# Reordering TensorE and the opening of a Mamba scan stage: eight weight parts, softplus behind the second gate, the second batch's rows normalized sooner

## The reference

```python
xz = layernorm(x) @ W_in.T                      # 512 -> 2 * 1024
x_proj, z = split(xz)
x_conv = silu(conv_b + causal_conv4(x_proj))
x_dbl = x_conv @ W_xproj.T                      # B (16), C (16), dt (1)
dt = clip(softplus(x_dbl[..., -1]), 0.001, 0.1)
h_t = exp(dt_t * A) * h_(t-1) + dt_t * B_t * x_conv_t ;  y_t = sum(h_t * C_t)
y = y * silu(z) + x_conv * D_param
x1 = x + y @ W_out.T
```

## Time and profile before

| | |
|---|---|
| median of 3 runs | 2617.36 us (2613.93 to 2620.7) |
| profiled execution, its own time | 2616.86 us |
| its span, first to last instruction | 2615.2 us |
| PE busy | 2416.5 us, 92% of the span |
| DVE, ACT, POOL busy | 57%, 46%, 25% |
| mean granted PE clock | 0.969 |

### The profile page before, as it was taken

One profiled execution on the slowest core, in us unless ns is written; L12 is line 12 of the kernel. 1 busy time (PEld: TensorE's weight loads), 2 busy tenths in 40 slices (PEclk: granted clock), 3 DMA queues, 4 the chain that ended last, 5 costly groups with the idle time before them and its releaser, 6 DMA issues. The chain is left out here.

```text
span 2615.2 us, 47758 instructions
## 1 busy us (share of the span) xinstructions
PE 2416.5 (92%) x16951; PEld 2128.4 (81%) x16951; DVE 1492.4 (57%) x2583; ACT 1199.3 (46%) x1912; POOL 648.2 (25%) x1040
## 2 busy tenths in 40 slices
PE   5999999999997899999999983499999999999997
PEld 5899898998996688888888862288888888888886
DVE  5877877777774466666666655644334334333332
ACT  6655555655653444444444431044344444434342
POOL 3111111211214444444453521112030311203021
PEclk9999999999998999999999986699999999999999
DMA  4111111111115666666666532124241523424221
GB/s 122 48 37 42 47 38 39 47 38 47 40 39 160 168 182 175 180 181 178 179 162 186 154 102 84 52 89 112 93 108 65 140 74 105 119 80 108 84 65 20
DMA packets 236833, 261.01 MB, mean 100 GB/s; under 512 B 70312, under 2 KB 160424, under 8 KB 236560
## 3 DMA queue, kind: packets, MB, share of 16 engines
q1 hardware_dynamic: 195600, 237.48, 31.1%
q0 software_dynamic: 40960, 20.41, 4.4%
HBM read 182.47 MB, written 68.80 MB: 96 GB/s over the span
## 5 line engine op out<-in xcount | busy, mean ns | idle before, releaser
L420 PE MATMUL a_psP<-s_xnT_h,s_w_l 128*128 128x256 f32 x1024 | 298.5, 292 | 27.2 <-DVE s_xnT_l L667 17.0
L2243 DVE TENSOR_TENSOR d_h_l<-d_hf,d_h_h 128x616 fp32r<-128x616 f32 x124 | 99.2, 800 | 392.3 <-ACT d_h_h L2067 392.3
L1972 PE MATMUL d_psH<-d_xgT_h,d_w_l 128*128 128x308 f32 x1024 | 314.5, 307 | 3.0 <-ACT d_hf L2103 2.0
L1973 PE MATMUL d_psH<-d_xgT_l,d_w_h 128*128 128x308 f32 x1024 | 311.5, 304 | 0.0
L1974 PE MATMUL d_psH<-d_xgT_h,d_w_h 128*128 128x308 f32 x1024 | 311.3, 304 | 0.0
L2103 ACT ACTIVATE d_hf<-d_psH,d_b1c 128x308 f32<-128x308 f32 x256 | 130.7, 518 | 383.5 <-PE d_psH L1974 382.6
L421 PE MATMUL a_psP<-s_xnT_l,s_w_h 128*128 128x256 f32 x1024 | 290.9, 284 | 0.0
L422 PE MATMUL a_psP<-s_xnT_h,s_w_h 128*128 128x256 f32 x1024 | 290.5, 284 | 0.0
L1939 POOL DMA_INDIRECT out_dram<-d_ob,d_to x40 | 103.7, 2593 | 686.0 <-ACT d_ob L2120 675.9
L1972 PE MATMUL d_psO<-d_w_h,d_h_l 128*123 128x512 f32 x620 | 244.2, 394 | 0.0
L1973 PE MATMUL d_psO<-d_w_l,d_h_h 128*123 128x512 f32 x620 | 244.0, 394 | 0.0
(11 more groups left out here) (378 smaller groups left out, 6062.7 us busy)
## 6 DMA issues: line engine op xcount, KB each, us to landing
d_w<-in_W_dram SPq DMA_DIRECT2D x64, 1024.0 KB, 6.1
b_qst<-qs_d SPq DMA_DIRECT2D x48, 512.0 KB, 6.6
b_kst<-ks_d SPq DMA_DIRECT2D x48, 512.0 KB, 6.6
s_raw<-in_x_dram SPq DMA_DIRECT2D x16, 512.0 KB, 3.5
s_xres<-in_x_dram SPq DMA_DIRECT2D x16, 512.0 KB, 3.6
x_d<-s_xres SPq DMA_DIRECT2D x16, 512.0 KB, 2.8
s_raw<-in_ctxT_dram SPq DMA_DIRECT2D x16, 512.0 KB, 9.5
s_xres<-x_d SPq DMA_DIRECT2D x16, 512.0 KB, 9.3
```

Source lines behind the costliest of these rows:

```text
L420: pe.matmul(out, lo_w, hi_x, start=first, stop=False)
L1972: pe.matmul(out, lo_w, hi_x, start=first, stop=False)
L1973: pe.matmul(out, hi_w, lo_x, start=False, stop=False)
L2243: dve.tensor_tensor(out, a, b_, ALU.subtract).then_inc(done, 1)
```

## The change

Five edits, all in `mamba_phase`:

1. **PE's order at the seam of two bodies.** `out_proj(7)` of a body moves from between the two `turn_rows` to the next body, behind the M matmuls and ahead of the wait for `xnT_lo`. In bodies 0, 1 and 16 there is none to move in front (body 16 takes that of body 15, and does its own at its end).
2. **PE's order in the middle**, for bodies with `prev` and `cur`: before x_dbl(5), y(0), x_dbl(6), z(0), x_dbl(7), y(1), z(1); after y(0), x_dbl(5), z(0), x_dbl(6), y(1), x_dbl(7), z(1).
3. **ACT**: softplus moves from the front of d = 1 to its end, behind `y_hi(1)` and the silu of z(1).
4. **The opening**: eight weight parts in five staging tiles (`xres` and the joined `t1`/`y2` tile are added); only parts 5, 6 and 7 reuse one. Parts 6 and 7 are issued behind the load of batch 1. ACT and DVE take part 1 after the rows of batch 0. ACT does one silu on a constant row ahead of tile 0. POOL's four pieces move to tiles 2 to 5. PE does 3 and 5 matmuls of a constant (`busy`) around the first transposes.
5. **Body 0 on DVE**: `moments(1)` at d = 2 and `normalize(1)` at d = 3.

```diff
-        place = [0, 1, 2, 1, 1, 1]
-        early = [t.rearrange("p a b -> p (a b)") for t in (xc[0], xc[1][:], zs[:])]
+        early = [t.rearrange("p a b -> p (a b)") for t in (xc[0], xc[1][:], zs[:], xres[:], ty[:])]
+        place = [0, 1, 2, 3, 4, 1, 3, 4]
+        rows_of = [(0, 2), (2, 2), (0, 2), (2, 1), (3, 1), (0, 4), (4, 2), (6, 2)]
...
+            for c in range(3, 5):
+                part(c)
+
+            sp.wait_ge(stg_h, 2)
+            sp.wait_ge(stg_l, 2)
+            part(5)
+
+            def last_parts():
+
+                sp.wait_ge(stg_h, 5)
+                sp.wait_ge(stg_p, 5)
+                part(6)
+                part(7)
...
                 elif cur:
                     sp.dma_start(xl, x_v[b + 1]).then_inc(x_ld, 16)
+                    if isinstance(b, int) and b == 0:
+                        last_parts()
...
-                        if isinstance(b, int) and b == 0 and i < 4:
-                            gate_lo(3, (i // 2, slice(i % 2 * (E // 2), (i % 2 + 1) * (E // 2))))
+                        if isinstance(b, int) and b == 0 and i >= 2 and i < 6:
+                            gate_lo(3 + (i - 2) // 2, slice(i % 2 * (E // 2), (i % 2 + 1) * (E // 2)))
...
+            def busy(n):
+
+                for _ in range(n):
+                    pe.matmul(psO[0][:, 0:S + P], ident[:], mask[:], start=True, stop=True)
+
             pe.wait_ge(setup_pool, 8)
             pe.wait_ge(setup_dve, 1)
+            busy(3)
             for h in range(2):
                 turn_rows(0, h)
+            busy(5)
...
+                if prev and not (isinstance(b, int) and b == 1):
+
+                    out_proj(b - 2, KE - 1)
                 if cur:
                     pe.wait_ge(xnT_lo, 2 * b + 2)
                     for i in range(KE):
                         in_proj(i, i, x_mm)
                         if i >= 3:
                             x_dbl(i - 3)
-                    x_dbl(KE - 3)
+                    if not prev:
+                        x_dbl(KE - 3)
...
                     if cur and d == 0:
-                        x_dbl(KE - 2)
+                        x_dbl(KE - 3 if prev else KE - 2)
+                    if cur and prev and d == 1:
+                        x_dbl(KE - 1)
                     if cur:
                         in_proj(9 + 2 * d, KE + d, z_mm)
+                    if cur and prev and d == 0:
+
+                        x_dbl(KE - 2)
...
-                for h in range(2):
-                    if prev:
-                        out_proj(KE - 2 + h)
-                    if cur:
+                if prev:
+                    out_proj(b - 1, KE - 2)
+                if cur:
+                    for h in range(2):
                         turn_rows(b + 1, h)
+                else:
+                    out_proj(b - 1, KE - 1)
...
+                        weights_hi(1)
                         weights_hi(2)
+
+                        act.wait_ge(setup_dve, 1)
+                        act.activation(dt_r[:, 0:1], ones_row[:, 0:1], ACT.Silu)
...
-                        if isinstance(b, int) and b == 0 and i == 0:
-                            weights_hi(3)
+                        if isinstance(b, int) and b == 0 and i in (2, 3):
+                            weights_hi(1 + i)
...
-                    if isinstance(b, int) and b == 0 and d in (2, 4):
-                        weights_hi(KD + d // 2 - 1)
+                    if isinstance(b, int) and b == 0 and d in (2, 4, 6):
+                        weights_hi(4 + d // 2)
...
                         act.activation(zs[:, d, :], psP[(9 + 2 * d) % 3][:, 0:S], ACT.Silu).then_inc(z_rdy, 1)
+                    if cur and d == 1:
+
+                        act.wait_ge(rows_a, 3 * b + 3)
+                        ch = Chain(act, exps_a, 2, b)
+                        ch.did(act.activation(dt_r[:], dt_r[:], ACT.Exp))
+                        ch.wait()
+                        ch.did(act.activation(dt_r[:], dt_r[:], ACT.Ln, bias=1.0))
...
-                        if first and d in (3, 5):
-                            weights_lo(KD + d // 2 - 1)
+                        if first and d in (3, 4, 6):
+                            weights_lo(5 + d // 2 - 1)
...
-                        if d == 5:
+
+                        if d == (2 if first else 5):
                             moments(b + 1)
+                        if first and d == 3:
+                            normalize(b + 1)
                         if d == 7:
                             rows_3()
-                            normalize(b + 1)
+                            if not first:
+                                normalize(b + 1)
```

More of the change, by code:

```diff
@@ L485, in x_dbl, with out_proj @@
                              i == 0, i == KE - 1).then_inc(xd_mm, 1)
+                def out_proj(yb, d):
+                    pe.wait_ge(y2_lo, 8 * yb + d + 1)
+                    if d == 0:
+                        wait(pe, res, 2 * yb)
+                    for t in range(TT):
+                        c = slice(t * P, t * P + P)
+                        mm = split_mm(psO[t][:], y2_h[:, d % 2, c], y2_l[:, d % 2, c], wout_h[:, d, :], wout_l[:, d, :],
+                                      d == 0, d == KE - 1)
+                    mm.then_inc(o_mm, 1)
                 if prev:
@@ L532, in body @@
                 for d in range(KE):
-                    if cur and d == 1:
+                    if cur and not prev and d == 1:
                         x_dbl(KE - 1)
@@ L561, in weights_hi @@
             def weights_hi(c):
-                act.wait_ge(stg[place[c]], 16 * place[:c + 1].count(place[c]))
+                act.wait_ge(*landed(c))
                 copy(chunks[c][0], stage[c], stg_h)
-            for c in range(KD // 2):
-                weights_hi(c)
+            weights_hi(0)
             def body(b, par, prev, cur):
```

91 lines of the change are left out of this document (38 added, 53 removed).

## The result

The changed kernel takes 2589.99 us (median of 4 runs, 2588.22 to 2593.34) against 2617.25 for the kernel before in the same series (4 runs). The ratio is 0.99, with a 95% interval of 0.9886 to 0.9914: faster by 1.0%. The profiled execution took 2590.91 us and its span is 2589.3. The forecast was 2589 (2580 to 2601).

The account below looks back on a forecast made before the run. PE was taken to pace the steady bodies, and a chain of transfers, copies and waits body 0. Savings of 11.9 (seam), 9.75 (middle) and 7 (body 0), 28.7 us from 2616.86, gave a forecast of 2589, range 2580 to 2601.

Parts of the forecast that it names:

- the two waits named: Steady body: PE waits at the seam for the transposed rows (0.76 us) and mid-body for POOL's `xcr_l` (1.13 us).
- The term of 11.9: Seam: moving `out_proj(7)` saves 0.85 us at each of 14 seams, bodies 2 to 15, 11.9 us in all.
- the two meet: Seam: DVE's rows end at 261.8 as PE is ready at 261.9, so `in_proj` starts then instead of 262.77.
- The gain in the middle: Middle of a body: under PE's new order z(1) starts 0.8 us sooner, with a wait of 0.3 left before x_dbl(7).
- The stall of y(4): Middle: y(4) waits 0.15 us for the later silu of z(2), leaving 0.65 us a body, 9.75 us in all.
- The cover is used up exactly: Middle: z(2)'s silu comes 2.1 us later, just when y(4) needs it; further ACT delay is paid 1 for 1.
- takes nothing away: Softplus on ACT: edit 3 only moves work, with no gain of its own.
- Rival B: Middle gains nothing: ACT some 0.8 us later than chained, y(4) waits for z(2)'s silu; 2598 us, chance 0.20.
- the fifth result: Body 0, DVE: `rows_2(0)`'s fifth result comes at about 44.3 us instead of 45.45, 1.1 sooner.
- the 7.0 us: Body 0: batch 1's first product comes at 63.0 instead of 70.13 us; bounds 2 and 12 us.
- Here SP decides: Body 0: row copies, held in SP's queue by the last weight part, go at 44.4; `rows_2(2)` starts 8.4 us sooner.
- only moves forward: Phase behind body 16's barrier: untouched by the change, so it starts sooner, with no gain counted in it.

Follow-up runs that it names:

- act_reordered: Changed kernel with ACT's silu of z(1) ahead of `y_hi(1)` and `xt_hi_(3)` ahead of the last gate's silu: 2585.95 us.
- softplus_back: Changed kernel with softplus put back at its old place, at the front of d = 1 (edit 3 undone): 2598.27 us.
- two_more_loads: Changed kernel with one more exp and ln behind softplus in bodies 1 to 15, for their two table loads: 2656.41 us.
- middle_alone: Kernel before with edit 2 alone, softplus at its old place: 2618.23 us, ratio 0.9986 to 1.0012.
- opening_alone: Kernel before with edits 4 and 5 alone, softplus at its old place: 2613.62 us.
- normalize_late: Changed kernel with edit 5 undone, `moments(1)` at d = 5 and `normalize(1)` at d = 7 in body 0: 2593.34 us.
- gate1_first: Changed kernel with ACT's silu of z(1) ahead of `y_hi(1)` in bodies 1 to 15: 2587.33 us.
- all_three: Changed kernel with both ACT reorderings (silu of z(1), `xt_hi_(3)`) and DVE's small weights moved behind tile 1's convolution: 2585.46 us.

## Why the prediction was right, and where it was not

**What bounds the kernel.** Right. PE sets the pace of a steady body, and the two waits named were the ones to be had: 18 us of waits in the steady bodies before by the profile's view of waits, 1.2 after, beside y(4)'s 0.27 a body, which that view leaves out.

**Edit 1.** The mechanism is as told: the second `turn_rows` directly behind the first, M, `out_proj(7)` as cover, no wait. The term of 11.9 is over-sized: 10.0 us in the fifteen intervals. The step that failed is "the two meet" at every seam. At one seam in two DVE's subtractions come later, and PE waits 0.25 us for them. DVE's gap before it (297.87 to 298.27) stands only at these seams; as two bodies are one turn of the loop, the jump back is a likely cause, but this wasn't tried by itself. Act_reordered shows that the gap costs PE nearly nothing once the work ahead of it is sooner.

**Edits 2 and 3.** The gain in the middle was worked out as 0.8 and is 0.72. The stall of y(4) was put at 0.15 and is 0.27. Together 0.45, by the difference of periods 0.56 (softplus_back: 0.49), where 0.65 was forecast: 8.4 us against 9.75. "The cover is used up exactly" was right, and two_more_loads shows what lies behind it. What the prediction lacked is that edit 2 needs edit 3. It priced softplus as a step that "takes nothing away", and counted 0.8 for PE's order alone. middle_alone had 0, since y(3) then waits for the silu of z(1). Rival B (the middle gains nothing) was therefore real, with another wait than it named, and it was edit 3 that kept it out.

**Edits 4 and 5.** 5.4 us against 7.0. The copies left the queue at once, and the distance from them to the first product was forecast as 63.0 - 44.4 = 18.6 and is 64.74 - 46.77 = 18.0. Two things in the account were wrong.

The step that failed is the one ahead of the copies, the fifth result "at about 44.3": it came at 46.49. The chain took PE to be at full clock throughout, and left out the lock between DVE's casts and POOL's rest. By the table of body 0 the clock from 35 to 40 us is 1.3 of it (45.16 with the same program at full clock) and the lock 1.4 (43.73 without it as well), together more than the 2.2 that were missing. So the 7.0 us missed by 1.6, of which the clock of this one execution is 1.3. At the full clock edits 4 and 5 gave 5.4 (opening_alone, 64.6) and softplus's place 1.3 more (63.3), a share of body 0 that the prediction didn't give to edit 3.

"Here SP decides" is only half shown. In the kernel before, the last weight part held the copies in SP's queue until 51.48, and held ACT until 56.14 and DVE behind ACT. The copies need some 7.7 us from the first issue until they are there (normalize_late), so they were there by about 59.2 (an estimate from 51.48), and DVE was not free until 61.37. Taking the part out of the queue alone would thus have gained at most what ACT and DVE let through. The eight parts ended both waits, and no run separates them. The remaining parts of the edit are not needed for the gain: `busy` and edit 5 are worth nothing here, though both changed the trace as described.

**The table loads.** The prediction weighed the Trainium skill's 2.66 us for a switch against the rows and took 1.28. two_more_loads settles it for this kernel: two loads and two activations took 2.91 us. By the Trainium skill's ScalarE: Activation LUTs, What ACT_TABLE_LOAD costs, the loads alone would have been 5.3 (an estimate, twice its 2.66).

**The rest of the time.** The prediction took the next phase as one that "only moves forward". It moved by 23.2 us and was 4.1 shorter. This brought the total to where the sum had put it. Of the 4.1 us, 3.6 lie between two instructions of PE in the last part of the phase. Timeline of PE, in the changed kernel, then in the kernel before:

```profile
1537.95 0.74 PE L1317 MATMUL b_psT<-b_qst,b_kst 104*128 104x256 f32 x4 [0.64 <-ACT b_PT L1497]
...
1567.32 1.54 PE L1357 MATMUL b_psT<-b_ident,b_xn 128*128 128x128 f32 x8 [4.60 <-DVE b_xn L1598]
```

```profile
1561.35 0.93 PE L1272 MATMUL b_psT<-b_qst,b_kst 104*128 104x256 f32 x4 [0.64 <-ACT b_PT L1452]
...
1594.34 1.97 PE L1312 MATMUL b_psT<-b_ident,b_xn 128*128 128x128 f32 x8 [4.61 <-DVE b_xn L1553]
```

That is 29.4 us against 33.0, with waits in between that are as long in both but for one (1.42 against 1.75). What differs is PE's clock. Busy time by stretch, the changed kernel first:

```profile
1540.00:1570.00 30.00, 17.50 (x111) 11.34 (x110) 9.65 (x17) 5.10 (x6) 2.43 (x3) 0.79 0.09 36
```

```profile
1563.20:1593.20 30.00, 19.43 (x109) 12.61 (x109) 8.66 (x15) 4.22 (x6) 2.62 (x3) 0.67 0.05 18
```

The same two instructions are 29.4 us apart in gate1_first too, and 33.0 to 33.1 in normalize_late and act_reordered. In all_three it is 31.4, with 0.67 in its 30 us as well, so the granted clock of a stretch is not the whole measure. Why the clock is granted sooner in one execution than in another stays open, and no experiment was made on it. So the gain of the change is the 23.2 us; the further 2.7 are not to be put down to it.

## What to carry to other kernels

Before a step on the engine that sets the pace is moved forward, follow what it will wait for next: here the order on PE gave nothing until the activation behind which the next bank came free was moved as well, and each of the two edits measured alone would have been thrown away. Where a chain in the opening decides, look on DVE and POOL for short instructions beside a long one of the other engine, since a cast of 0.21 us can take 1.38. In a stretch where PE often waits, look at the granted clock before two single traces are compared: one program's body 0 differed by 1.3 us. Check each term of a forecast at a marker inside the trace, not in the total: this total was right to 1 us while its terms were 5.5 too high.

## What the runs showed of the hardware

- A wait of PE can cost more than itself. After some 3.07 us of idle time in each body, PE worked the next 3.2 us in one body (granted clock 0.51) and 6.4 us in another (0.52) at the 1.2 GHz level. Added waits of 2.8 us a body cost 4.62. The waits of 0.25 to 0.76 us in the bodies of the kernels before and after came with a granted clock of 1.00.
- A cast on DVE, or a small instruction on POOL, that started under a long subtraction of the other engine lasted until that one ended: 1.38 us for 0.21, and 2.67 for 0.72.
- The same body 0 behind the same waits of PE had a granted clock of 0.66 in one execution and 1.00 in another, from 35 to 40 us (24 and 36 matmuls), and was 1.3 us longer in the first.
- The same code took 838.0 and 842.1 us in two kernels' executions, with granted clocks of 0.79 and 0.67 in a stretch of its last part. Over all the kernels it was 836.1 to 843.5.
